# Twelve record scatters on GpSimd, each behind a product of its own

## The reference, cut to what matters

```
x = layernorm(x + attn(x))            # 3 heads of width 512, softmax(QK^T)V, mean over heads, fc, bias
x = layernorm(x + xattn(x, ctx))      # 16 heads of 32, keys and values from ctx, causal
scores = softmax(x @ gate_w.T)        # 64 experts
topk_w, topk_idx = top_k(scores, 6)
# each expert takes its first 128 choices in token order:
buf[expert, pos] = x[token];  d = (silu(buf @ w_gate) * (buf @ w_up)) @ w_down
y[token] = sum over its 6 choices of topk_w * d[expert, pos]
y += (silu(x @ sh_gate.T) * (x @ sh_up.T)) @ sh_down.T
x = layernorm(x + y)
```

## Time and profile before

| | us |
|---|---|
| median of 3 runs | 2173.54 (2169.0 to 2173.59) |
| the profiled execution | 2161.73 |
| its span | 2160.0 |
| PE busy | 2016.5 (93%) |
| DVE busy | 1648.0 (76%) |
| ACT busy | 1030.0 (48%) |
| POOL busy | 735.9 (34%) |
| POOL: scatters of records, L167, 204 of them | 201.0 |

### The profile page before, as it was taken

How to read it: one execution, slowest core, us unless ns; L and a number is a source line. 1 busy time by engine, 2 the same in 40 slices (tenths; PEclk the granted TensorE clock), 3 DMA queues, 4 the chain that set the end, 5 groups by cost and what they waited for, 6 DMA issues and landing times. The chain is left out here.

```text
span 2160.0 us, 46058 instructions
## 1 busy us (share of the span) xinstructions
PE 2016.5 (93%) x16976; PEld 1227.8 (57%) x16976; DVE 1648.0 (76%) x3682; ACT 1030.0 (48%) x1569; POOL 735.9 (34%) x709
## 2 busy tenths in 40 slices
PE   8899999999999999999999997689999999999998
PEld 3566656665665565565565663345555555555553
DVE  5457877877877887887887887747887878688767
ACT  5325535434444453453453543435565565565645
POOL 1002223223223223223223221244465566555543
PEclk9999999999999999999999998899999999999999
DMA  6700011011011011011011003268999999999958
GB/s 234 57 23 31 24 52 51 0 51 51 0 51 51 6 45 51 10 41 51 10 41 51 33 28 126 64 194 250 273 294 285 297 286 288 258 292 299 284 103 313
DMA packets 134324, 267.24 MB, mean 124 GB/s; under 512 B 32699, under 2 KB 42939, under 8 KB 134236
## 3 DMA queue, kind: packets, MB, share of 16 engines
q1 hardware_dynamic: 110108, 226.06, 32.3%
q0 software_dynamic: 24128, 40.01, 9.5%
HBM read 208.67 MB, written 57.42 MB: 123 GB/s over the span
## 5 line engine op out<-in xcount | busy, mean ns | idle before, releaser
L167 POOL DMA_INDIRECT slot_table<-table_records,slot_of_choice x204 | 201.0, 985 | 401.3 <-PE ring L861 277.4
L861 PE MATMUL ring<-xT_split,tion_then_expert_weights 128*128 128x256 f16 x2304 | 270.0, 274 | 5.4 <-PEq L311 5.4
L861 PE MATMUL ring<-tion_then_expert_weights,xT_split 128*128 128x512 f16 x1152 | 259.7, 380 | 0.0
L831 POOL TENSOR_SCALAR_AFFINE_SELECT scratch<-scratch 128x1024 f32<-128x1024 f32 x64 | 70.5, 1101 | 544.3 <-ACT scratch L1108 544.3
L861 PEld LDWEIGHTS ring<-xT_split,tion_then_expert_weights 128*128 128x128 f16 x2304 | 222.8, 98 | 43.7 <-issue 13.8
L1092 ACT ACTIVATE scratch<-ring 128x512 f16<-128x512 f32 x224 | 131.1, 595 | 211.0 <-PE ring L861 208.5
L1583 POOL DMA_INDIRECT expert_sums<-tion_then_expert_weights,scatter_index x64 | 137.8, 2154 | 188.4 <-PE moe_bank L1635 52.1
L861 PEld LDWEIGHTS ring<-tion_then_expert_weights,xT_split 128*128 128x128 f16 x1152 | 109.1, 98 | 132.6 <-issue 8.1
L1225 DVE CUSTOM_DVE_ANT_0 quad<-quad,causal_penalty 128x128 f32<-128x128 f32 (+1 forms) x512 | 164.9, 394 | 14.0 <-PE quad L951 11.0
L1186 DVE SCALAR_TENSOR_TENSOR scratch<-ring,scratch 128x512 f16<-128x512 f32 x192 | 129.2, 684 | 51.5 <-ACT scratch L1092 51.5
L1635 PE MATMUL moe_bank<-w_down_split,hidden_T_split 128*128 128x512 f16 x576 | 136.7, 383 | 4.5 <-DVE hidden_T_split L1845 4.5
(11 more groups left out here) (246 smaller groups left out, 4019.9 us busy)
## 6 DMA issues: line engine op xcount, KB each, us to landing
gate_up_landing<-in_w_gate SPq DMA_DIRECT2D x43, 704.0 KB
gate_up_landing<-in_w_up SPq DMA_DIRECT2D x43, 704.0 KB
scratch<-in_w_down SPq DMA_DIRECT2D x43, 512.0 KB
scratch<-in_w_gate SPq DMA_DIRECT2D x21, 704.0 KB
scratch<-in_w_up SPq DMA_DIRECT2D x21, 704.0 KB
tion_then_expert_weights<-in_w_down SPq DMA_DIRECT2D x21, 512.0 KB
scratch<-in_w_down SPq DMA_DIRECT2D x43, 192.0 KB
xT_in<-in_xT SPq DMA_DIRECT2D x16, 512.0 KB
```

The costliest lines, as they stand in the source:

```text
L167: pool.indirect_dma_start(self.dram, bass.IndirectOffsetOnAxis(ap=self.slot[:, tb, c:c + 1], axis=0), self.record[:, tb, c, :], None, boun ...
L831: pool.affine_select(out=p32[:, g % 2, :, 0:2 * P], in_=p32[:, g % 2, :, 0:2 * P], compare_op=ALU.is_ge, fill=0.0, base=0, pattern=[[0, 4] ...
L861: last = pe.matmul(out_, left(a, c), right(b, c), start=(n == 0 and not onto), stop=(n == 3 * chunks - 1))
```

## The change

GpSimd's list names each scatter of the loop's bodies and of body 16 by itself (count 1), and each waits for a product of its own: one of the body before (-1, `last_job`) or of this one (0, `job`). There is one list for the bodies of the loop and one for body 16. The tail keeps its single step of twelve without such waits, and the expert stage isn't changed.

```diff
+SCATTERS = [("SC", n, 1) for n in range(NB * TOPK)]
+SCATTER_BEHIND = [
+    (-1, ("V", 2, 1)), (-1, ("O", 0, 0)), (-1, ("O", 1, 0)), (-1, ("OUT", 1, 0)), (0, ("C", 0, 0)), (0, ("V", 0, 0)),
+    (0, ("V", 0, 1)), (0, ("Y", 0, 1)), (0, ("Q", 0, 0)), (0, ("S", 0, 1)), (0, ("Y", 1, 0)), (0, ("V", 1, 0)),
+]
+SCATTER_BEHIND_LAST = [
+    (-1, ("V", 2, 1)), (-1, ("O", 0, 0)), (-1, ("O", 1, 0)), (-1, ("OUT", 0, 0)), (-1, ("OUT", 1, 0)), (0, ("K", 1, 0)),
+    (0, ("T", 1, 0)), (0, ("Q", 0, 0)), (0, ("Q", 1, 0)), (0, ("TX", 1, 0)), (0, ("R", 0, 0)), (0, ("C", 1, 0)),
+]
 POOL_BODY = [
-    ("XS", 0, 0), ("CS", 0, 0), ("SC", 0, 2), ("SC", 2, 2), ("SC", 4, 1), ("SC", 5, 1), ("SC", 6, 1), ("SC", 7, 1),
-    ("SC", 8, 1), ("SC", 9, 1), ("SC", 10, 1), ("SC", 11, 1), ("MASK", 0, 0), ("MASK", 1, 0), ("MASK", 2, 0), ("MASK", 3, 0),
+    ("XS", 0, 0), ("CS", 0, 0),
+] + SCATTERS + [
+    ("MASK", 0, 0), ("MASK", 1, 0), ("MASK", 2, 0), ("MASK", 3, 0),
 ]
...
-SCATTER_BEHIND = {2: ("C", 0, 0), 4: ("V", 0, 0), 5: ("V", 0, 1), 6: ("Y", 0, 1), 7: ("T", 1, 0), 8: ("C", 1, 0),
-                  9: ("K", 0, 0), 10: ("Q", 0, 0), 11: ("Q", 1, 0)}
-POOL_LAST = [
-    ("CS", 0, 0), ("SC", 0, NB * TOPK), ("MASK", 0, 0), ("MASK", 1, 0), ("MASK", 2, 0), ("MASK", 3, 0),
+POOL_LAST = [("CS", 0, 0)] + SCATTERS + [
+    ("MASK", 0, 0), ("MASK", 1, 0), ("MASK", 2, 0), ("MASK", 3, 0),
 ]
...
                     elif name == "SC":
                         if g == 0:
                             pool.wait_ge(rec_ready, b.n(0, 0, 1, 1))
-                        else:
-                            pool.wait_ge(full, b.job(*SCATTER_BEHIND[g]))
+                        if count == 1:
+                            body, job = (SCATTER_BEHIND_LAST if b.is_(B) else SCATTER_BEHIND)[g]
+                            pool.wait_ge(full, b.last_job(*job) if body else b.job(*job))
                         own_wait(pool, taken)
                         table.scatter(pool, g, count)
```

## The result

The changed kernel took **2109.2 us** (median of 3 runs, 2100.8 to 2110.75) against 2173.54 before: ratio 0.9702 (95% interval 0.9669 to 0.9736), 3% faster. The direction and the main mechanism were forecast, the size came out larger. The profiled execution took 2100.8 us with a span of 2099.0, 61.0 us less than the span before.

A forecast was written before the change was run, and what follows sets the result against it. TensorE, busy 93% of the span, was taken to set the pace, so only its idle time could be won. 42.3 us (loop) + 2 (body 16) = 44.3, off the 2173.5 median: 2129 us, range 2112 to 2170.

The forecast's parts named there:

- step 6: Tail and expert stage: their twelve scatters in a row are not touched, so 0 gain.
- step 5: Body 16: issuing its twelve scatters apart wins 2.5 us before OUT0, less a possible first-mask wait; taken as +2.
- Step 1: Loop bodies 2 to 15: without the scatter burst beside R, Q1 starts 3.02 us earlier, 42.3 us in all.
- Steps 2 and 3: Loop: scatters at their new places cost 0; the later twelfth scatter still lands before records are overwritten, cost 0.
- D: Loop's score products M0 to M3: scatters moved among them delay news, 23 us slower overall, 2196; chance 0.10.
- Step 4: Loop, scatters 0 and 1 beside AV3: they stay, so AV3's late news and OUT0's 1.45 us wait stay; gain 0.
- rival E: Loop, at AV3: its late news goes as well, 14 x 1.45 us more, 2109; chance 0.06.
- Rival C: Loop, at R: no gain, 2173; late news belongs to transfers, R itself or recorded executions only; chance 0.13.

The follow-up runs named there:

- e1: Changed kernel with the loop's scatters 6 to 11 back behind their earlier products, four in a row beside R; chip 15: 2161.25 us, ratio 0.9937.
- e4: Changed kernel with the loop's scatters 8 to 11 all behind Q0, a burst beside slower products; chip 15: 2128.1 us, ratio 0.9783.
- e3: Changed kernel with the first scatters moved clear of AV3, in the loop and body 16; chip 15: 2092.15 us, ratio 0.9613.
- e10: The changed kernel again, no edit, profiled on chip 7: 2086.08 us, ratio 0.9971 to the kernel before.
- e5: Changed kernel with the loop's scatter 7 behind C1, a lone one beside R; chip 3: 2082.61 us, ratio 0.9983.
- e11: Changed kernel with a lone scatter beside R in the loop, run again on chip 7: ratio 1.001.
- e13: Changed kernel with a lone scatter beside R in the loop, third run, on chip 8: ratio 0.9981.
- e16: Changed kernel with a lone scatter beside R in the loop, fourth run, on chip 8: ratio 0.9997.
- e8: e3's kernel with the tail's twelve scatters split, eight at once and four behind R; chip 3: 2090.5 us, ratio 1.0021.
- e15: e3's kernel with the tail's twelve scatters split into eight and four, run again on chip 8: ratio 1.0001.
- e2: Changed kernel with body 16's twelve scatters in a row as before, the loop as changed; chip 15: 2116.89 us, ratio 0.9741.
- e9: The kernel before the change, no edit, profiled on chip 7: 2082.68 us.

## Why the prediction was right, and where it failed

Three terms of the sum were too small: step 6, the expert stage, was put at 0 without any width and came out 8.6 us shorter; step 5, body 16, was put at +2 and gave 5.7; and the half clock behind the late news, 4.2 us, was in no step. The paragraphs below take the steps one by one.

**Step 1, the burst beside R.** Right in place and size, where the news is late: 14 x 3.02 = 42.3 us. e1 undoes it. The cause as the prediction words it, scatters back to back, is too wide, as V00's row shows.

**Steps 2 and 3, the moved scatters and the record buffer.** Right at 0: the waits for the maxima are 0.2 and 0.3 us at the longest, and the record steps begin 7.1 us behind the twelfth scatter's end (613.24 to 620.34) without a wait. That D wasn't empty, e4 shows: where the score products meet a burst instead of lone scatters, they pay 1.05 us a body. The Trainium skill's 2 us for such a transfer (DMA: Bandwidth & Descriptors, Anatomy of one DMA — SWDGE path) agrees as far as rows go: in e4 the packets are through 1.74 us after the scatter's start (609.00 to 610.74); the receipt isn't shown. The prediction counted those 2 us from the scatter's end; from its start, the estimate by that page is 1 us earlier. The Trainium skill's rule of the port pair (SBUF — State Buffer, two separate sides) names VectorE instructions in a two-port mode or with two SBUF inputs. No row here tests it, for the split reads one input from a PSUM bank: beside scatters, at 608.61 in e4, it takes 0.69 us as elsewhere.

**Step 4, AV3's late news stays.** Right: 1.6 us on VectorE and 1.5 ahead of OUT0, as before. So rival E fell, and e3 shows what it was worth: 1.67 us a body. That the time, 2109, is just E's number is chance.

**Step 5, body 16.** Mis-sized: +2, measured 5.7. The step compared with a loop body's end, where a pair holds AV3. Ahead of body 16 GpSimd comes to scatter 0 early enough that scatter 1 has to wait for O0, so AV3 meets one lone scatter. AV3, scatters 0 and 1, its reader and OUT0 in the changed kernel:

```profile
1246.63 1.00 POOL L167 DMA_INDIRECT slot_table<-table_records,slot_of_choice  x1 [0.15 <-issue]
...
1251.22 0.50 PE L1002 MATMUL ring<-scratch,ones 128*32 128x256 f16 x16
...
1251.64 0.97 POOL L167 DMA_INDIRECT slot_table<-table_records,slot_of_choice  x1 [4.02 <-PE ring L870]
...
1252.94 1.76 DVE L1250 RECIPROCAL inv_denominator<-ring 128x256 f32<-128x256 f32 x1 [0.62 <-PE ring L1002]
...
1256.21 5.34 PE L870 MATMUL ring<-wout_split,scratch 128*128 128x512 f16 x24 [0.18 <-DVE scratch L1255]
```

AV3 ends at 1251.72 and is read at 1252.94, 1.2 us later, with the lone scatter beside it: the row need not have two. From AV3's end to OUT0 it is 4.5 us against 8.25, where 5.76 was taken. Another 1.4 us were lost before by a stretch at half clock behind that wait (1306.0 to 1309.4). The half us set against it for the first mask wasn't paid: GpSimd waits there for ScalarE.

**The term that was missing, in the loop.** The burst beside R leaves TensorE with pauses in Q0 or ahead of K1 and one ahead of Q1, and now and then the clock falls behind them. The kernel before at 1012 us, the granted clock third from the end, and Q1 there:

```profile
1012.00:1016.00 4.00, 3.54 (x18) 2.48 (x19) 3.45 (x6) 0.00 (x0) 0.19 (x1) 0.57 0.01 0
```
```profile
1012.46 4.43 PE L861 MATMUL ring<-x1T_split,xwq_split 128*128 128x256 f16 x24 [1.43 <-DVE k_split L1186]
```

Q1 takes 4.43 us instead of 2.79, much of it at 1.2 GHz. Between 200 and 1240 us, of twenty profiled executions, two show such stretches: this one (one) and e1's (two), the only two in which R's news is late. A second one at 1251.4 in the kernel before, behind R of body 15, and one body of 79.4 us with no such stretch make up nearly all of the 4.2 us. The profile page, with its clock in 40 slices, doesn't show them singly.

**Step 6, the expert stage.** Its 8.6 us can't be put down to the change. From its first to its last matmul it took 742.3 us before, 733.8 after, and 736.5 to 759.4 in the other eighteen profiles, with stretches at half clock that come and go; the kernel before alone took 742.3 once and 752.2 once. The failure was to give this stage no width at all: with 8.6 us of it, the range would have held the time.

The sum: 42.3 + 4.2 + 5.7 + 0.2 = 52.4 us lie ahead of the expert stage, where 44.3 were forecast; the other 8.6 us are within what executions differ by. That the medians differ by 64.3 and not 61.0 (or 52.4) is not taken apart here.

**Rival C** had a part without a condition of its own: the late news "exists only in an execution that is recorded". It isn't the recording, for the timed runs differ by as much between chips (2174.55 and some 2086 us) as the profiles' bodies do (14 x 4.7 = 66 us, and body 16 and the tail). It goes with the chip, or with a state that it keeps through a batch of runs; the runs can't tell the two apart. By the medians of e10, the changed kernel is worth nothing there (2086.08 against 2087.03).

**What stays open.** What makes the news late on one chip and not on another, for it couldn't be chosen; what besides a scatter it takes, for V00 passes beside a row of three while AV3 is held by one, and matmul length is only a guess from these rows; whether a lone scatter beside R holds news (e5, e11, e13 and e16 met no chip on which anything is held); and whether e8's split of the tail would gain on chip 15. On chip 15, e3's kernel is the fastest (0.9613, where the changed one had 0.9702 in its own timing, whose chip isn't on record); on the others all are alike. I would keep e3's lists: they cost nothing where the news is prompt (e15, 1.0001).

## What to carry to other kernels

Read the trace for a product that ended long before its reader starts, and look for what ran in between; several such places with one companion are worth a change of order even if the engine named looks idle. Before such a gain is believed, measure both kernels on more than one chip: here a change is worth 3% in its first timing and nothing on chip 7, and one edit of it cost 52 us on chip 15 and nothing on chip 8. Give stages that the change doesn't touch the width that they show from one execution to the next.

## What the runs showed of the hardware

- Scatters of GpSimd can delay what TensorE tells. From a product's end to its reader it is 1.2 us beside one (AV3 ahead of body 16, after), 2.5 us beside a pair and 3.7 beside four (before), 8.0 beside twelve (e2, chip 15). ScalarE's news in such a stretch passed at once (e4).
- Not every product is held: V00, of 512-column matmuls, ends beside a row of three and is read 0.04 us later (before).
- TensorE's own matmuls pause beside the burst too: 9.0 us in 17 pieces in 430 to 1250 us (before), in e1 0.34 and 0.75 us within one Q0.
- No other transfers are needed for it: AV3's pair and e4's burst run with the DMA engines busy 0.01 of the time.
- Chips 3, 7 and 8 show none of it with the same instructions, 0.97 us a scatter and 0.30 us between two (e9).
- Two pauses of TensorE, the first of 0.5 to 0.8 us and the second of 1.4 to 2.1 us, are sometimes followed by a stretch of 3.4 us at 1.2 GHz (before, e1); in the other eighteen executions, without the pauses at R, the clock doesn't fall between 200 and 1240 us.
